# Expert tiles listed by the batch of their first row, with gathers, two batch sums and key preparation moved beside other work

## The reference

```
x = x + L0_xattn(norm(x), ctx)      # layer 0
x = x + L0_ffn(norm(x))             # layer 1: 8 experts, each row takes 1
x = x + L1_xattn(norm(x), ctx)      # layer 2
x = x + L1_ffn(norm(x))             # layer 3: 16 experts, each row takes 3 and weighs them
x = x + L2_xattn(norm(x), ctx)      # layer 4, causal mask
x = x + L2_ffn(norm(x))             # layer 5
x = x + L3_xattn(norm(x), ctx, mask)# layer 6
x = x + L3_ffn(norm(x))             # layer 7
```

## Time and profile before

| | us |
|---|---|
| runs (3) | 649.23, 650.31, 650.84; median 650.31 |
| the profiled execution | 652.92, of which its span 651.1 |
| PE busy | 449.9 (69% of the span) |
| DVE busy | 341.3 (52%) |
| ACT busy | 238.6 (37%) |
| POOL busy | 212.5 (33%) |

### The profile page before, as it was taken

One profiled execution on the slowest core, in us unless ns is written; L12 is line 12 of the kernel. 1 busy time (PEld: TensorE's weight loads), 2 busy tenths in 40 slices (PEclk: granted clock), 3 DMA queues, 4 the chain that ended last, 5 costly groups with the idle time before them and its releaser, 6 DMA issues.

```text
span 651.1 us, 9752 instructions
## 1 busy us (share of the span) xinstructions
PE 449.9 (69%) x2682; PEld 359.2 (55%) x2682; DVE 341.3 (52%) x1182; ACT 238.6 (37%) x628; POOL 212.5 (33%) x269
## 2 busy tenths in 40 slices
PE   3787866999058886400799899255379999996940
PEld 3664653999026775400687885023257677784730
DVE  4635364554146765320243444453567576867885
ACT  1111001666034642100476663123225654573511
POOL 5101173000460145775000004767352034463014
PEclk9985556999668995555799998776578999999655
DMA  7399972121840000111233331111000000000002
GB/s 200 58 375 346 403 307 65 49 66 34 264 137 2 0 21 30 48 53 49 83 102 106 99 106 50 49 49 38 16 20 2 0 2 2 1 1 1 1 1 65
DMA packets 58969, 53.68 MB, mean 82 GB/s; under 512 B 11458, under 2 KB 45203, under 8 KB 58788
## 3 DMA queue, kind: packets, MB, share of 16 engines
q1 hardware_dynamic: 52708, 43.62, 20.8%
q0 software_dynamic: 4096, 8.40, 4.1%
q10 hardware_dynamic: 2112, 1.05, 0.5%
HBM read 24.20 MB, written 28.84 MB: 81 GB/s over the span
## 4 chain that ended last, share of the span: by engine, by line
PE 39%; issue 27%; DVE 15%; ACT 5%; DVEq 4%; POOL 3%; DMA 3%; SPq 2%; another core or an unknown queue 1%; ACTq 0%; POOLq 0%
PE bank L1907 8%; PE bank L1894 7%; PE bank L1776 4%; PE bank L1792 2%; PE bank L1781 2%; ACT xn L1377 2%; SPq L345 2%; PE bank L1858 2%; POOL rstd L488 2%; DMA h_sb<-rowbuf 1%; PE bank L1886 1%; PE bank L1707 1%; PE bank L1624 1%; PE bank L1620 1%; DVE x L1064 1%
## 5 line engine op out<-in xcount | busy, mean ns | idle before, releaser
L1468 ACT ACTIVATE r<-bank,b 128x128 f32<-128x128 f32 x224 | 68.0, 367 | 28.8 <-PE bank L1894 28.7
L500 POOL DMA_INDIRECT rowbuf<-h_sb,slots x64 | 62.3, 973 | 29.9 <-issue 17.8
L1907 PE MATMUL bank<-wall,r 128*128 x448 | 68.5, 284 | 1.2 <-ACT r L1468 1.2
L487 POOL TENSOR_SCALAR nmr<-mv 128x4 f32<-128x4 f32 x32 | 7.9, 248 | 172.6 <-DVE veps L628 164.7
L511 POOL DMA_INDIRECT vZ<-rowbuf,slots x40 | 38.6, 964 | 73.0 <-DMA rowbuf<-h_sb 61.7
L1907 PEld LDWEIGHTS bank<-wall,r 128*128 128x128 f32 x448 | 57.3, 192 | 5.1 <-issue 2.1
L1894 PE MATMUL bank<-on,e_sb 128*128 128x128 f32 x352 | 53.6, 281 | 4.8 <-ACT on L1461 2.2
L1764 PE MATMUL bank<-ident,xn 128*128 128x128 f32 x64 | 13.5, 348 | 58.7 <-ACT xn L1377 58.5
L1075 DVE TENSOR_TENSOR h_sb<-bank,b2all 128x128 f32<-128x128 f32 x88 | 25.6, 291 | 52.2 <-PE bank L1907 52.0
L1792 PE MATMUL bank<-vB,eT 128*128 128x36 f32 x384 | 50.5, 281 | 2.1 <-ACT eT L1396 2.1
L1792 PEld LDWEIGHTS bank<-vB,eT 128*128 128x128 f32 x384 | 50.6, 206 | 2.2 <-ACT eT L1396 2.2
(11 more groups left out here) (259 smaller groups left out, 935.4 us busy)
## 6 DMA issues: line engine op xcount, KB each, us to landing
rowbuf<-zero SPq DMA_DIRECT2D x17, 1024.0 KB, 11.5
wall<-in_w SPq DMA_DIRECT2D x4, 2048.0 KB, 17.2
h_sb<-rowbuf SPq DMA_DIRECT2D x88, 64.0 KB, 1.8
rowbuf<-h_sb SPq DMA_DIRECT2D x88, 64.0 KB, 1.6
x<-in_x ACTq DMA_DIRECT2D x4, 256.0 KB, 5.5
rowbuf<-h_sb,slots POOLq DMA_INDIRECT x64
b2all<-in_L_ffn_b SPq DMA_DIRECT2D x1, 1024.0 KB
out<-h_sb SPq DMA_DIRECT2D x4, 256.0 KB, 2.6
```

Source lines behind the costliest of these rows:

```text
L500: nc.gpsimd.indirect_dma_start(rowbuf[0:MOE[l][0] * REGION * P], bass.IndirectOffsetOnAxis(slots[:, k * T + t:k * T + t + 1], 0), tile_of( ...
L1468: i = a.activation(hT[:, (u % 2) * 512 + c * P:(u % 2) * 512 + (c + 1) * P], bank[2 + u % 2][:, c * P:(c + 1) * P], ACT.Relu, bias=b1[l][: ...
L1907: y = mm(bank[6 + u % 2][:, 0:P], hT[:, (u % 2) * 512 + c * P:(u % 2) * 512 + (c + 1) * P], wall[:, bass.ds(e * n + (WHALF + c * P), P)], ...
```

## The change

1. `slot_list` sorts tiles by (batch of the tile's first row, expert) instead of by expert. `route` keeps the running counts of each batch (`seen`). The list takes 31 DVE instructions where it took 13. Two constant tables are loaded (`segs1`, `segs3`).
2. `gather(l, b)` waits only for the first `READY[l][b]` tiles: 12, 16, 20, 24 for layer 1; 28, 40, 52, 64 for layer 3. No row of batch b lies in a later tile.
3. In layer 1 `add_experts(1, 0)` and its statistics run on DVE at slot 21 of the loop. In layer 3 the sums of batches 0 and 1 run at slots 47 to 50 and 59 to 62, one choice of three per slot; `normed`, `turn_x` and `turned` of batch 0 run at slots 55, 57, 59. Batches 2 and 3 are added in periods 2 and 7 of layer 4.
4. `prepare(4, .)` runs between the routing of batches 2 and 3 of layer 3, `prepare(6, .)` between `slot_list(3)` and the loop. `prepare(4, .)` uses other PSUM banks (2 and 6).

```diff
+ADDED = {2: {3: 2, 6: 3}, 4: {2: 2, 7: 3}}
+TURNED = {2: {0: 1, 4: 2, 7: 3}, 4: {0: 1, 3: 2, 8: 3}}
+READY = {l: [-(-(((b + 1) * W * P * TOPK[l] + MOE[l][0] * (P - 1)) // P) // GT) * GT for b in range(B)] for l in MOE}
...
-            def gather(l, b, part):
+            def gather(l, b, first, last):
 
                 K = TOPK[l]
-                if b == 0 and part == 0:
+                if first == 0:
                     for r in range(2):
-                        pool.wait_ge(s_ys[r], 16 * GT * (tile_before[l] + SLOT_TILES[l]) // BODY)
+                        groups = sum(1 for g in range(READY[l][b] // GT) if g % 2 == r)
+                        pool.wait_ge(s_ys[r], 16 * GT * (tile_before[l] // BODY + groups))
...
+            gather(1, 0, 0, 4)
+            gather(1, 1, 0, 4)
             power(8)
+            gather(1, 2, 0, 4)
             power(9)
+            gather(1, 3, 0, 4)
...
+            gather(3, 0, 0, 12)
+            gather(3, 1, 0, 8)
             power(16)
+            gather(3, 1, 8, 12)
             pool.wait_ge(s_a, 4 * len(AL))
+            gather(3, 2, 0, 6)
             power(17)
+            gather(3, 2, 6, 12)
+            gather(3, 3, 0, 4)
             power(18)
+            gather(3, 3, 4, 12)
...
                 # slot_list, new parts
+                for h in range(2):
+                    v.tensor_tensor(wide.rearrange("p (s m) -> p s m", m=8), rows.unsqueeze(2).to_broadcast([NS, G, 8]),
+                                    full[0:NS, 8 * h:8 * h + 8].unsqueeze(1).to_broadcast([NS, G, 8]), ALU.is_gt)
+                    dve.drain()
+                    v.tensor_reduce((tiles, hot)[h], wide.rearrange("p (s m) -> p s m", m=8), AX_X, ALU.add)
+                    dve.drain()
...
+                for b in range(B):
+                    summed = xn[0:NS, (b % 2) * 256:(b % 2) * 256 + E * E].rearrange("p (e f) -> p e f", e=E)
+                    v.tensor_tensor(summed, by_batch(2)[:, b].unsqueeze(1).to_broadcast([NS, E, E]),
+                                    upto[:, :].rearrange("p (e f) -> p e f", e=16)[0:NS, 0:E, 0:E], ALU.mult)
+                    dve.drain()
+                    v.tensor_reduce(by_batch(3)[:, b], summed, AX_X, ALU.add)
...
                 # DVE, beside(l, s), inside the expert loop
+                    if s == 21:
+                        add_experts(1, 0)
+                        stats_of(norm_no(2, 0), 0)
                 else:
...
+                    for b, at in enumerate((47, 59)):
+                        if s == at:
+                            dve.wait_ge(s_gat[b], landed[3])
+                        if at <= s < at + 3:
+                            add_choice(b, s - at)
+                        if s == at + 3:
+                            stats_of(norm_no(4, b), b)
...
                 # DVE, before the loop of layer 3 (PE the same; ACT: prepare(2 * b, .) after copy_logits(b), b = 2, 3)
+            gating(3, 2)
+            route(3, 2)
+            for stage in range(6):
+                prepare(4, stage)
+            gating(3, 3)
+            route(3, 3)
             slot_list(3)
+            for stage in range(6):
+                prepare(6, stage)
+            v.copy_predicated(cap6[:, :], mask_u8[:, :], neg3[:, :])
             moe(3)
...
                 # ACT and PE, inside the loop of layer 3
+                        if l == 3 and s == 55:
+                            normed(4, 0)
+                        if l == 3 and s == 59:
+                            turned(4, 0)
...
+                        if l == 3 and s == 57:
+                            turn_x(4, 0)
```

More of the change, by code:

```diff
@@ L143, in build @@
         base0, base = sb("base0", 16), sb("base", 16)
[L144 to L148, removed]
+        seen = sb("seen", B * 16)
+        segs = {l: sb(f"segs{l}", 3 * B * MOE[l][0]) for l in MOE}
         at_f = sb("at_f", 2)
+        rest_f = sb("rest_f", 2)
+        place_f = sb("place_f", 2)
         of_f = sb("of_f", 2)
@@ L366, in _ @@
             load(s_c1, full[:, :], A["full"])
+            load(s_c1, segs[1][:, :], A["segs1"])
+            load(s_c1, segs[3][:, :], A["segs3"])
             load(s_c1, number[:, :], A["number"])
@@ new lines, in part, with by_batch @@
+                def part(i, n=G):
+                    return ab[0:NS, i * 64:i * 64 + n]
+                def by_batch(i):
+                    return part(i).rearrange("p (b e) -> p b e", b=B)
+                rows, tiles, fresh, ends, hot = (part(i) for i in range(5))
+                reached, table = ab[0:NS, 320:320 + 2 * G], r5[0:NS, 0:2 * G]
+                total = part(7, B)
+                wide = xn[0:NS, 0:G * 8]
+                index, start, of = (segs[l][0:NS, i * G:(i + 1) * G] for i in range(3))
@@ L1111, in moe @@
                     add_bias(SLOT_TILES[l] - 2 + u, BODY - 2 + u, experts[u])
-                if l == 3:
-                    for later in (4, 6):
-                        for stage in range(6):
-                            prepare(later, stage)
-                    v.copy_predicated(cap6[:, :], mask_u8[:, :], neg3[:, :])
-                add_experts(l, 0)
-                stats_of(4 * l + 4, 0)
             def v_loads(src, E):
@@ L1491, in moe @@
                 relu(SLOT_TILES[l] - 1, BODY - 1, experts_of(SLOT_TILES[l] + 1, 1)[0])
-                if l == 3:
-                    for later in (4, 6):
-                        for stage in range(5):
-                            prepare(later, stage)
-                normed(l + 1, 0)
-                turned(l + 1, 0)
+                if l == 1:
+                    normed(2, 0)
+                    turned(2, 0)
             def gate_exp():
@@ L1513, in _ @@
                 copy_logits(b)
+                for stage in range(5):
+                    prepare(2 * b, stage)
             moe(3)
@@ L1931, in moe @@
                 second(last, BODY - 1, False, experts[1])
-                if l == 3:
-                    for later in (4, 6):
-                        for stage in range(5):
-                            prepare(later, stage)
-                turn_x(l + 1, 0)
+                if l == 1:
+                    turn_x(2, 0)
             for stage in range(5):
@@ L1949, in _ @@
             project(2, 3)
-            for b in (2, 3):
-                turn_x(3, b)
-                logits(3, b)
-                ranks(3, b)
+            turn_x(3, 2)
+            logits(3, 2)
+            ranks(3, 2)
+            for stage in range(5):
+                prepare(4, stage)
+            turn_x(3, 3)
+            logits(3, 3)
+            ranks(3, 3)
             slot_list(3)
+            for stage in range(5):
+                prepare(6, stage)
             moe(3)
@@ L2076, in constants, with segments @@
     e = np.arange(16)
+    def segments(E):
+        i = np.arange(B * E)
+        return np.tile(np.concatenate([i, i % E * REGION, i % E]).astype(f), (P, 1))
     return {
```

131 lines of the change are left out of this document (57 added, 74 removed).

## The result

The kernel after the change takes 629.01 us (median of 4 runs, 627.94 to 632.75), the one before 650.53 (4 runs, 649.23 to 650.84): ratio 0.968, 95% interval 0.964 to 0.973. The forecast was 588, in 576 to 606. The sign was right and the size wrong: 21.5 us came, 62 were forecast.

What follows compares the result with a forecast made beforehand. Bound by waits (PE 39% of the chain), with three standstills around loops 1 and 3; two attacked. 651.1 + 4.7 + 0.5 - 19.0 - 1.5 + 0 + 6 - 56.9 + 3 = 587.9 span; 588 forecast as median, range 576 to 606.

Steps and rivals of the forecast that it cites:

- Loop 3: Loop 3: DVE's sums lose 2.3 us twice, ACT's norms and PE's turns 1, loads 1: +6, bounds +2 and +17.
- The gaps: Gaps like 1.84 and 4.98 us in old layer 4, nobody working, may recur elsewhere: +3, bounds 0 and +7.
- List and start of loop 1: Before and in loop 1: longer tile list +4.7 us, sum and statistics on DVE in the loop +0.5.
- Behind loop 1: Between loop 1 and layer 2: batch 0 already summed, so first scores and maximum come earlier: -19.0 us.
- The clock: First 20 us of layer 2: less idleness gives back part of PE's lost clock: -1.5 us, bounds 0 and -4.
- Before loop 3: Before loop 3: longer list and moved preparations hidden under POOL's scatters: 0 us, bounds 0 and +3.
- Layer 4: Layer 4: power of batch 3 ends 36.1 us behind loop 3, not 93.0: -56.9, bounds -50 and -60.
- Rival 1: Loop 3: gathers crawl beside DVE's copies, 5 us each, so DVE waits at slots 47 and 59: 609 us, chance 0.07.
- rival 4: Lists fail: tile order or a wait keeps gathers behind the loop: 645 us, chance 0.02.
- Rival 3: Loop 3: SP's issues take 1.59 us instead of 0.33 while POOL generates descriptors: 662 us, chance 0.03.

Runs made afterwards that it cites:

- dummy_small: Kernel before plus 30 spare indirect gathers of 4 bytes a row, in bursts in loop 3: 635.34 us, beside 638.67 for the kernel before.
- dummy_gap: Kernel before plus 30 spare gathers in loop 3's bursts, a POOL memset of 128x256 before each: 660.58 us, loop 3 90.2 us.

## Why the forecast was wrong, point by point

- **Loop 3: +6, measured +37.4. This is the step that failed.** It priced DVE's sums, ACT's norms and the tile loads, each about rightly: without gathers the loop takes 82.5, and PE's waits for loads are only 3.2 us in the loop (2.6 before). It gave the gathers no price except through DMA engines and POOL's own pace. Their price, 1.13 to 1.25 us each when issued back to back, is that of late signals. The bounds (+2 to +17) missed it, and no rival has it.
- **The gaps: +3, bounds 0 to +7.** I saw 1.84 and 4.98 us of "unknown" in the chain, said that nobody works in them and took a few as a constant. That was misread: PE works in them until 453.46 and from 455.06 to 457.99, and what is lost is the wait for its late signals. They lay in a burst of gathers, and the change moves 30 gathers beside a loop of short steps that wait for each other. Even at their full length, priced per gather (6.8 us over the 12 around it is 0.6), these rows would have said +17 for 30.
- **List and start of loop 1: +4.7 + 0.5.** The list takes 7.7 us (98.98 to 106.65) instead of 2.7, +5.0, and the loop's first product starts at 117.41, +3.5, the scatters having ended 1.7 earlier by chance. The loop lost 2.9, not 0.5, beside two bursts of four (4 to 5 in later runs; paced, it takes 52.1). A late product near the loop's end, and the first scores behind it:

```profile
164.60 1.15 PE L1950 MATMUL bank<-wall,r 128*128 x8 [2.31 <-ACT r L1510]
...
173.29 1.10 PE L1821 MATMUL bank<-VW,xnT_all 128*128 128x512 f32 x2 [1.25 <-ACT xnT_all L1433]
```

- **Behind loop 1: -19.0.** Scores now start at 173.29, the first maximum at 174.58 (187.14 before): -12.6 with +6.4 lost until the loop's end, so -19.0. Right. The clock was to give 1.5 more in layer 2; from there to the first scatter of layer 3 it is 0.9.
- **Before loop 3: 0, bounds 0 to +3.** The list is as worked out, 281.96 to 292.55, and hidden. But prepare(4) was not quite: slots came 5.2 us after POOL was free, for the DVE step ahead of them waited for PE's ranks, done at 275.0, until 280.55, again a signal of PE beside a burst (of scatters). It comes 3.4 us behind the last scatter's end (277.13), so a late signal can outlast its burst.

```profile
280.55 0.22 DVE L899 TENSOR_TENSOR slot_at<-bank,base 128x64 f32<-128x64 f32 x1 [7.92 <-remote]
```

```profile
282.32 0.95 POOL L507 DMA_INDIRECT rowbuf<-h_sb,slots  x1 [5.19 <-DVE slots L909]
```

  Net: the first scatter of layer 3 is 13.5 us earlier, loop 3 starts 10.5 earlier, +3.0 lost, at the bound.
- **Layer 4: -56.9 (bounds -50 to -60).** rstd(19) ends at 462.0, 40.0 us behind the loop's end (93.0 before, 36.1 forecast): -53. Within the bounds; with the gathers behind the loop it is 91.0. The clock of PE there was to be near 1.00; from 422 to 450 it is 0.82.
- **The sum**: the forecast erred by 38 us against the profiled span: 31.4 in loop 3, 3.0 before it, about 2 in layers 1 and 2, 4 in layer 4, 1 behind it, less the 3 allowed for gaps.
- **Rival 1** (gathers crawl beside DVE's copies) did not happen: gathers stay at 0.94 to 0.95 us, 1.25 apart (0.99 to 1.07 for the first one or two of a burst). The stronger test is dummy_small, whose loop runs at full pace with one copy of 0.29 us a tile beside twelve gathers: they are busy 11.27 us, 0.94 each. The Trainium skill (SBUF — State Buffer, "SBUF: two separate sides") gives some 3100 ns for such a transfer beside a copy of a length that it doesn't state, and says that it stays blocked until the copy has ended, plus some 115 ns; for a copy of 0.29 us that would be 0.4 us at the most, an estimate from that page. There the trace shows at most 0.1 us more, so the 3100 ns doesn't carry over to copies this short. The harm goes the other way: from POOL's transfers to the others. Of the rivals' times, 645 (rival 4) lies nearest to 629, 609 (rival 1) next, both for a reason that did not hold. Rival 3 (SyncE's issues) did not happen either.

Shown: that gathers in the loop, not sums, order or volume, cost it; that spacing them by 0.3 us takes three quarters of the price away; that it happens on four of the five chips that the experiments ran on. Only argued: that a signal waits for POOL to pause its descriptor work, which rests on where late signals arrive in dummy_gap; one that came 3.4 us behind a burst speaks against a plain form of it. Open: whether an execution that isn't recorded has late signals too. Every run here was recorded, and in bursts 26 to 49% of the update records of PE, ACT and DVE are missing in the changed kernel's trace (at most 2% on the chip without late signals), so the recording may take part. Not tried: the changed kernel on the chip without late signals, where 588 may have been near; plain transfers by POOL on a chip with them; and spaces under 0.3 us, or a space between the scatters of the routing.

## What to carry to other kernels

Before indirect transfers are moved beside a loop of short steps that signal each other, price each one that is issued back to back at its full distance (here 1.1 to 1.25 us), and leave a space between them: a wait per tile or 0.3 us of other work on POOL took the price to 0.3 to 0.4. A chain of waits that names "an unknown queue" in a kernel of one core is a finding, not noise: look which engine runs a burst there, and price it per transfer of that burst. Such holes can hold work of another engine, so read its timeline as well. And compare variants only beside each other on one chip: the 30 gathers of 4 bytes a row cost the loop 2 us on one and 33 on another.

## What the runs showed of the hardware

- In bursts of indirect transfers by POOL 1.25 us apart, many of PE's semaphore updates come over 0.5 us late (17 to 38% in the kernel before, 28 to 55% after, by the way of pairing), by up to some 5 us. ACT's recorded ones never do, DVE's only at three places of a kernel at the most. Outside bursts they come 0.01 us after the end.
- It hardly depends on volume (1.11 us a gather with 4 bytes a row, 1.24 with 512), and a busy POOL alone (memsets of 1.0 us) doesn't cause it (loop 3 81.1 us).
- The transfers themselves are not late: in loop 3 the last packet of a burst lands 1.1 to 1.4 us after its last instruction's end where the loop beside it is held up, and 1.4 to 1.8 where it is not (dummy_small).
- One chip shows none of it, and the unchanged kernel is 11 to 15 us (2%) faster there (one run, 638.67 us).
- Idle time caused so costs twice: PE's granted clock fell to 0.50 inside a burst (1.2 of 2.4 GHz) in a stretch where PE was busy 2.90 us, behind one where it was busy 5.77, and four 128x128 products that take 0.68 us took 1.20.
